# A graph-attention layer: a ring of seven weight tiles, denominators in runs of three, and an output tile staged in three parts

## The reference

```python
x_l = (x @ W + b).reshape(N, NHEADS, C)              # 4096 x 8 x 64
alpha_l = jnp.einsum('nhc,hc->nh', x_l, att_l)
alpha_r = jnp.einsum('nhc,hc->nh', x_l, att_r)
scores = alpha_l[:, None, :] * alpha_r[None, :, :]   # i x j x head
scores = jnp.where(adj[:, :, None] > 0, scores, NEG_INF)
att = jax.nn.softmax(scores, axis=1)                 # over j
out = jnp.einsum('ijh,jhc->ihc', att, x_l)
```

## Time and profile before

| what | value |
|---|---|
| median of 3 runs | 3698.03 us (3696.79 to 3701.27) |
| the profiled execution | 3698.87 us, span 3697.2 us |
| PE / DVE / ACT / POOL busy | 94% / 79% / 68% / 42% of the span |
| `attend_gat` on TensorE | 359.74 to 1639.62 us of the span |
| values L562 | 4096 records, 923.4 us busy |
| denominators L571 (from the ring) | 3072 records, 369.4 us busy |
| exponentials L533 / masking L546 | 1024 each, mean 1228 / 1220 ns |

### The profile page before, as it was taken

How to read it: one execution, slowest core, us unless ns; L and a number is a source line. 1 busy time by engine, 2 the same in 40 slices (tenths; PEclk the granted TensorE clock), 3 DMA queues, 4 the chain that set the end, 5 groups by cost and what they waited for, 6 DMA issues and landing times. The chain is left out here.

```text
span 3697.2 us, 57761 instructions
## 1 busy us (share of the span) xinstructions
PE 3490.7 (94%) x22247; PEld 1388.7 (38%) x22247; DVE 2926.3 (79%) x2984; ACT 2527.1 (68%) x2432; POOL 1535.9 (42%) x1154
## 2 busy tenths in 40 slices
PE   6887999999999999987699999999999999999986
PEld 4554222222222222225344444444444444444433
DVE  6666999999999999978577777777777777777768
ACT  4455999999999999963466666666566666666642
POOL 2222101111011000110467767667776677766761
PEclk9988999999999999985799999999999999999995
DMA  8987677777767767668899999999999999999987
GB/s 289 315 302 254 154 159 157 154 158 168 159 156 158 160 155 164 148 160 270 189 201 202 198 204 205 205 200 199 201 204 206 204 201 196 203 206 204 194 186 246
DMA packets 371005, 729.39 MB, mean 197 GB/s; under 512 B 27024, under 2 KB 215440, under 8 KB 354368
## 3 DMA queue, kind: packets, MB, share of 16 engines
q0 software_dynamic: 99408, 419.90, 58.2%
q1 hardware_dynamic: 236096, 270.91, 23.9%
q10 hardware_dynamic: 35248, 35.14, 2.9%
HBM read 263.50 MB, written 59.69 MB: 87 GB/s over the span
## 5 line engine op out<-in xcount | busy, mean ns | idle before, releaser
L1151 DVE TENSOR_TENSOR a_weights<-a_psS,maskT 128x1024 f32<-128x1024 f32 x1024 | 1206.2, 1220 | 465.1 <-ACT a_psS L1115 465.1
L1115 ACT ACTIVATE a_psS<-a_psS,shift_bc 128x1024 f32<-128x1024 f32 x1024 | 1071.5, 1084 | 688.8 <-PE a_psS L1041 688.7
L546 DVE TENSOR_TENSOR g_weights<-g_weights,maskT 128x1024 f32<-128x1024 f32 x1024 | 1170.1, 1220 | 113.0 <-ACT g_weights L533 113.0
L533 ACT ACTIVATE g_weights<-al_bc,shift_bc,g_xl 128x1024 f32<-128x1024 f32 x1024 | 1167.9, 1228 | 91.4 <-PE g_psD L571 87.9
L1041 PE MATMUL a_psS<-a_q,a_k 128*64 128x512 f16 x8192 | 971.7, 380 | 19.3 <-DMA a_q<-q_scratch 18.6
L1058 PE MATMUL a_psO<-a_weights,a_v 128*64 128x512 f32 x4096 | 961.2, 592 | 0.0
L562 PE MATMUL g_psO<-g_weights,g_xl 128*64 128x512 f32 x4096 | 923.4, 598 | 11.3 <-DVE g_weights L546 11.3
L1174 POOL TENSOR_TENSOR a_pool_total<-a_pool_total,a_weights 128x1024 f32<-128x1024 f32 x336 | 918.2, 2733 | 0.0
L1041 PEld LDWEIGHTS a_psS<-a_q,a_k 128*64 128x64 f16 x8192 | 463.1, 110 | 648.3 <-issue 300.9
L1182 POOL DMA_DIRECT2D a_dma_total<-a_weights x480 | 456.3, 951 | 397.6 <-DVE a_weights L1151 209.8
L562 PEld LDWEIGHTS g_psO<-g_weights,g_xl 128*64 128x64 f32 x4096 | 277.8, 137 | 648.0 <-issue 518.1
(11 more groups left out here) (124 smaller groups left out, 1271.6 us busy)
## 6 DMA issues: line engine op xcount, KB each, us to landing
a_dma_total<-a_weights POOLq DMA_DIRECT2D x512, 512.0 KB, 5.3
g_total<-g_weights POOLq DMA_DIRECT2D x128, 1024.0 KB, 7.8
adj_sb<-in_adj_dram SPq DMA_DIRECT2D x128, 512.0 KB, 5.9
g_xl<-xl_scratch SPq DMA_DIRECT2D x127, 260.0 KB, 5.0
a_k<-k_scratch SPq DMA_DIRECT2D x256, 128.0 KB, 5.4
a_v<-in_L_gnn_v_dram SPq DMA_DIRECT2D x128, 256.0 KB, 4.0
al_bc<-alpha_scratch SPq DMA_DIRECT2D x32, 512.0 KB, 6.4
f_oT<-o_scratch SPq DMA_DIRECT2D x16, 1024.0 KB, 6.6
```

Of the source, the lines that this page charges most:

```text
L533: nc.scalar.activation(w[:, u % RING, h, :], al_bc[:, g % 2, h, :], ACT.Exp, bias=shift_bc[:, 0, g % PAIRS * 2 + h:g % PAIRS * 2 + h + 1], ...
L546: nc.vector.tensor_tensor(w[:, u % RING, h, :], w[:, u % RING, h, :], maskT[:, j, (g // PAIRS) * IC:(g // PAIRS + 1) * IC], ALU.mult).then ...
L1115: nc.scalar.activation(psS[n % RING][:], psS[n % RING][:], ACT.Exp, bias=shift_bc[:, 1, g % PAIRS * 2 + h:g % PAIRS * 2 + h + 1], scale=SC ...
L1151: nc.vector.tensor_tensor(w[:, u % NP, h, :], psS[n % RING][:].rearrange("p a c -> p (a c)"), maskT[:, j, (g // PAIRS) * IC:(g // PAIRS + ...
```

## The change

The ring has seven tiles instead of six. TensorE's denominators come in two runs of three a block instead of three couples: after the values of tile 3 it counts tiles 0, 2 and 3, after tile 7 tiles 4, 6 and 7. `o_sb` and `d_sb` become one tile `out_sb` of 128 x 512, through which a group's output goes in three parts: the first half of `psO`, the second half, and `psD`. ACT takes the parts after the exponentials of tiles 4, 10 and 16 of the next group, each only when the part before it has been stored; SP stores them behind its loads of `kb` 3, 4 and 5. The semaphore counts follow.

```diff
-        RING = 6
+        RING = 7
-        COUPLES = {2: (0, 2), 4: (3, 4), 7: (6, 7)}
+        RUNS = {3: (0, 2, 3), 7: (4, 6, 7)}
...
-        o_sb = sb("g_o", [P, IC], F32)
-        d_sb = sb("g_d", [P, HALF], F32)
+        out_sb = sb("g_out", [P, HALF], F32)
...
-            return u // JB * len(COUPLES) + sum(j < u % JB for j in COUPLES) + 1
+            return u // JB * len(RUNS) + sum(j < u % JB for j in RUNS) + 1
...
-            def store(g):
+            def store(g, part):
                 ic, pair = g // PAIRS, g % PAIRS
-                sp.wait_ge(taken, 2 * g + 2)
-                sp.dma_start(o_dram[0, pair, :, ic * IC:(ic + 1) * IC], o_sb[:]).then_inc(stored, 16)
-                for hf in range(2):
-                    sp.dma_start(d_dram[0, pair * 2:pair * 2 + 2, ic * IC + hf * HALF:ic * IC + (hf + 1) * HALF],
-                                 d_sb[32 * hf:P:64, :]).then_inc(stored, 16)
+                cols = [slice(ic * IC + hf * HALF, ic * IC + (hf + 1) * HALF) for hf in range(2)]
+                sp.wait_ge(taken, 3 * g + part + 1)
+                if part < 2:
+                    sp.dma_start(o_dram[0, pair, :, cols[part]], out_sb[:]).then_inc(stored, 16)
+                else:
+                    for hf in range(2):
+                        sp.dma_start(d_dram[0, pair * 2:pair * 2 + 2, cols[hf]], out_sb[32 * hf:P:64, :]
+                                     ).then_inc(stored, 16)
...
-                    if kb == 3 and g > 0:
-                        store(g - 1)
-            store(GROUPS - 1)
-            sp.wait_ge(stored, 48 * GROUPS)
+                    if kb in (3, 4, 5) and g > 0:
+                        store(g - 1, kb - 3)
+            for part in range(3):
+                store(GROUPS - 1, part)
+            sp.wait_ge(stored, 64 * GROUPS)
...
-            def take(g):
-                act.wait_ge(closed, g + 1)
-                if g > 0:
-                    act.wait_ge(stored, 48 * g)
-                nc.scalar.activation(o_sb[:], psO[g % 2][:].rearrange("p a c -> p (a c)"), ACT.Copy).then_inc(taken, 1)
-                nc.scalar.activation(d_sb[:], psD[g % 2][:], ACT.Copy).then_inc(taken, 1)
+            def take(g, part):
+                if part == 0:
+                    act.wait_ge(closed, g + 1)
+                if part > 0 or g > 0:
+                    act.wait_ge(stored, 64 * g + 16 * part)
+                nc.scalar.activation(out_sb[:], psO[g % 2][:, part, :] if part < 2 else psD[g % 2][:], ACT.Copy
+                                     ).then_inc(taken, 1)
...
-                if j == 4 and g > 0:
-                    take(g - 1)
-            take(GROUPS - 1)
+                if j in (4, 10, 16) and g > 0:
+                    take(g - 1, j // 6)
+            for part in range(3):
+                take(GROUPS - 1, part)
...
-                    pe.wait_ge(taken, 2 * (g - 1))
+                    pe.wait_ge(taken, 3 * (g - 1))
...
-                if j % JB in COUPLES:
-                    for t in COUPLES[j % JB]:
+                if j % JB in RUNS:
+                    for t in RUNS[j % JB]:
```

## The result

The changed kernel takes 3686.01 us in the median of 6 runs (3682.13 to 3686.44), the kernel before 3698.63 (3696.79 to 3701.27): a ratio of 0.9963, 95% interval 0.9951 to 0.9975. That is 12.6 us faster; 14 were forecast, with a range of 3681 to 3691. The profiled execution took 3686.04 us, span 3684.4.

The account below looks back on a forecast made before the run. TensorE, busy 1219.6 of 1220 us at full clock, was taken as the bound. From the profiled 3698.87 us, -18.7 for fewer changes and +4.7 at the stage's end gave 3684.9, or 3684 for the median; range 3681 to 3691.

Parts of the forecast that it names:

- TensorE bounds the stage: In most of the changed stage TensorE is busy 1219.6 of 1220 us, so a saving must shorten its own sequence.
- The price of a change: Between values and denominators TensorE pays 0.146 us each way; six changes a block become four, -18.7 us over 64 blocks.
- The ring: Seven tiles keep TensorE fed: slot free to tile usable takes 4.07 us, 1.08 us to spare; cost 0.
- (c): Rival: the ring starves TensorE at tiles 7 and 3 of the blocks; each further 0.1 us costs 12.8 us; chance 0.04.
- The parts inside the stage: ACT's three output copies of 0.58 us and SP's stores stay hidden inside the stage; cost 0.
- The end: At the stage's end the last group's copies, stores and landings run one behind the other, uncovered: +4.7 us.
- The start: The first run is 2.16 us longer while DVE fills the ring; a fourth tile needs no further wait: 0.
- (a): Rival: TensorE's rest goes with tiles or blocks, not changes, and stays; 3702.7 us; chance 0.05.
- (b): Rival: the last stores land as slowly as busy-stage loads, 8.8 us; +17.7 at the end, 3697.0 us; chance 0.05.
- (d): Rival: an ACT copy waits for its store in some groups; 1 us in half of them gives 3692 us; chance 0.04.

Follow-up runs that it names:

- experiment 1: Changed kernel with denominators back in couples after tiles 2, 4 and 7, ring of seven and three-part output kept; 3703.45 us, ratio 1.0013 to the kernel before.
- experiments 3 and 4: Against the changed kernel: 3, denominators 64 columns wide, 3993.47 us; 4, values in 32 columns, 3648.66 us, and the same with denominators in couples, 3648.26 us.
- experiment 5, e2_ring6: Changed kernel with only the ring back to six tiles; 3809.09 us, ratio 1.0298 to the kernel before.
- e4_narrow: Changed kernel with values multiplied in 32 stationary columns, four side by side; 3648.66 us, ratio 0.9863 to the kernel before.
- e6_wide: Changed kernel with denominators in 64 stationary columns, as wide as the values, into two PSUM banks; 3993.47 us.
- experiments 1, 2 and 4: Against the changed kernel: 1, denominators in couples, 3703.45 us; 2, in six runs of one, 3759.09; 4, values in 32 columns, 3648.66, with couples 3648.26.

## Why the prediction was right, point by point

**TensorE bounds the stage.** Right: it is busy for 1219.62 of 1220 us before and for 1200.00 of 1200 after, and every change of TensorE's sequence came out in the time.

**The price of a change, -18.7 us.** Right: -18.58 by the stage's ends, 18.34 by those of experiment 1, which is 0.143 to 0.145 us a change. The prediction called it a price for going between values and denominators. It is narrower: it is paid for the change of width between 64 and 32 columns (experiments 3 and 4). This gives the same sum here, but not the same remedy. The Trainium skill, TensorEngine Tiling (Array Packing), section Key Properties, says that changing the tiling mode drains TensorE, as against changing only the tile. These runs agree that the change of width costs time, 0.144 us each; the draining itself no trace shows.

**The ring, 0.** Right, with a chain 0.18 us too long: 3.89 us in experiment 5, so 1.26 us of cover, not 1.08. Rival (c) priced a starved ring at both halves of a block; with seven tiles TensorE never waits, with six it does so in both halves.

**The parts inside the stage, 0.** Right: by the instructions of tile `g_out` (what ended ACT's idle time before its copies: total, times), ACT's copies wait for a store twice in the whole stage, and both are the ones at its end.

```profile
  DMA o_scratch<-g_out: 4.2, 2
```

Inside the stage the list of waits has ACT waiting for TensorE's denominators alone, never for a DMA of `total`, so the slots freed by DMA were hidden as well. Copy 1 runs 19.0 us into the group (932.29 against 913.29, 19.0 worked out), store 0 is issued at 7.55 (7.5).

**The end, +4.7 us.** The mechanism is right, the term too large by 1.1: +3.61. A round of copy and store lasted 2.67 us (1624.38 to 1627.05) instead of 0.69 + 2.3 = 2.99, which is 0.6 of it in two rounds: each store of 256 KB took 2.05 us from issue to the next copy (1622.33 to 1624.38). The last two stores and the meeting took 2.50 us (1627.67 to 1630.17) instead of the 2.92 of the kernel before (1641.62 to 1644.54), 0.4 more. The estimate of 2.6 us a store from the Trainium skill, DMA: Bandwidth & Descriptors, section Anatomy of one DMA, was further off; the measured 2.05 decides.

**The start, 0.** Right, but the prediction read it wrongly: the 2.16 us by which the first run is longer are not DVE filling the ring. In the kernel before, TensorE had stood idle for 11.30 us; its granted clock is 0.50 (1.2 GHz) from its first values to 364.0 us and 1.00 (2.4 GHz) from 364.5 us on. Until then a weight load comes every 0.85 us instead of 0.43 (an idle time of 0.59 us before it instead of 0.27), and five such steps make 2.1 of the 2.16 us:

```profile
363.18 0.26 PEld L562 LDWEIGHTS g_psO<-g_weights,g_xl 128*64 128x64 f32 x2 [0.59 <-issue]
...
365.37 0.16 PEld L562 LDWEIGHTS g_psO<-g_weights,g_xl 128*64 128x64 f32 x2 [0.27 <-issue]
```

The changed kernel pays the same there (9.14 us against a steady 7.09).

**The rivals.** (a) and (b) fall by the rows above, (c) by the ring, (d) by the list of waits. What no step foresaw are the 2.2 us in the untouched work. Why the second attention's first loads landed later was not tried; by the scatter of the twelve traces there, and since the runs of one kernel spread by 4.3 us, the difference need not belong to the change. That the forecast of 3684 is only 2 us from the measured 3686 is thus in part luck: the end was forecast 1.1 us too dear, the untouched work came out 2.2 us longer, and the two partly cancel.

## What to carry to other kernels

When TensorE is full, read the starts of its runs, not its busy time: take the time of a run of three from that of a run of two, and what doesn't scale is a price of the change between them. Before such changes are made rarer, ask what in them costs: here the width of the stationary matrix, and the same work cut into four narrow matmuls instead of two wide ones paid nothing, and needed neither the deeper ring nor the new staging. And a tile reused through stores is free under other work but serial where a stage ends: give the last round tiles of its own.

## What the runs showed of the hardware

- Four f32 matmuls of 32 columns side by side take the time of two of 64 with the same moving columns: 6.87 us for four tiles of values in both widths (e4_narrow and e6_wide).
- A weight load isn't issued ahead across a change of width: 0.81 us idle ahead of it instead of 0.29 on the way to 32 columns, 0.84 on the way back to 64 (the changed kernel), and some 0.144 us of the matmuls' time lost for each change (the stage's lengths in experiments 1, 2 and 4).
- TensorE follows a finished mask by 0.06 us in the running stage (e2_ring6, 894.66 against 894.60).
